# Attention tiles of a fused two-layer kernel: the order of the fc1 and fc2 blocks on the tensor engine, from the third fc2 step on

## The chip, the cores and the metric

One core of one Trainium2 chip. The metric is the device time of one execution in microseconds, lower is better. The kernel before takes 2746.04 us, the median of three runs (2744.83 to 2759.59).

## What is computed

The input is (4, 384, 56, 56) in fp32. Layer 0 is a residual block with group norm, four depthwise convolutions, a sampled value tensor and a projection; the change does not touch it. Layer 1 is a second residual block on group-normed tokens, and its MLP part is where the change sits:

```python
xn = (xs - mu) / jnp.sqrt(var + EPS) * ln_g + ln_b
mid = jax.nn.silu(xn @ fc1_w + fc1_b) @ fc2_w + fc2_b     # 384 -> 1536 -> 384
qkv = (xs @ qkv_w)...                                     # 8 heads of 48
attn = jnp.einsum('bhld,bhle->bhde', k, v)                # q and k normalised
o = 0.5 * v + 1.0 / math.pi * jnp.einsum('bhld,bhde->bhle', q, attn)
o = o / jnp.linalg.norm(o, axis=-1, keepdims=True)
out = (o + mid) @ proj_w + proj_b
```

## The kernel before

The core works through four images (b = 0 to 3). Each image has a stage for keys and values and then seven attention tiles (t = 0 to 6) of 448 tokens; tile n = 7 b + t. Six tiles of images 0 to 2 and all seven of image 3 go through the function `tile`; the seventh of images 0 to 2 goes through `last_tile`, which also holds the output stage of layer 0 for the next image. So there are 25 executions of `tile` and 3 of `last_tile`.

Precision is kept by three passes: each fp32 operand is split into a high part (suffix H, rounded by ScalarE, ACT) and a low part (suffix L, the remainder, by VectorE, DVE), and a product is high times high, high times low, low times high (`three_pass`, lines 784 to 786, one matmul each).

The MLP of a tile is cut into twelve hidden chunks j of 128 (JC = 12). For each chunk:

- `fc1(n, j)` on the tensor engine (PE): nine matmuls into PSUM bank j % 2, from XRH and XRL. It first waits until S of step j - 2 has read that bank (semaphore `s_s`).
- `silu(n, j)` on ACT: S, one of two buffers, after fc1 step j and after the low split of step j - 2; then SH, the high part, one of three buffers, which must wait until fc2 step j - 3 has read it (semaphore `f2`).
- `split_s(n, j)` on DVE: SL, the low part, after SH.
- `fc2(n, j)` on PE: nine matmuls from SH and SL, three into each of banks 2, 3 and 4, in which all twelve steps are summed. It waits for SH and SL of step j.

PE runs fc1 ahead of fc2. `tile` issues fc1 steps 0 to 2, then fc2(0), fc1(3), fc2(1), fc1(4), fc2(2), fc1(5), and then a loop over i = 3 to 11. Between the blocks stand the small steps of the next tile, `pre` (transposes of X, the query matmuls, the query norms, the attention products), the transposes `turn_o` and `turn_unit`, and at i = 9 the output projection `proj` (27 matmuls), which sums into the same banks as fc2. `PRE` says at which i the steps of `pre` stand: the query norms (`query_norms`, 24 matmuls of 8 columns, line 1166) at i = 6, the attention products (`attend`, line 1180) at i = 7 and 8. At i = 5 stands `turn_o` (line 1235).

ACT and DVE run their own orders, written out by hand in the same way: silu steps among the norms, the query copies (line 1748), the copies MH of attended values (line 1772), and on DVE the splits among eight taps for each half of a convolution channel block (line 2395), the low parts ML (line 2369) and the head-wise scaling QQ (line 2345). Waits are on counting semaphores; each engine stops at the first instruction whose wait is not met.

The fc2 loop, word for word, is in the diff below.

Of the kernel before, what the change touches and what calls it, by code (L numbers as in the profile page):

```python
# [73 lines left out]
def build(nc, d, out):  # L74
# [22 lines left out]
    with ctx:  # L97
# [262 lines left out]
        def conv_unit(t, h):  # L360

            return 2 * t + h
# [387 lines left out]
        def _(pe):  # L750
# [31 lines left out]
            def three_pass(o, wh, wl, xh, xl, first, stop):  # L782

                mm(o, wh, xh, start=first, stop=False)  # L784
                mm(o, wh, xl, start=False, stop=False)  # L785
                return mm(o, wl, xh, start=False, stop=stop)  # L786
# [185 lines left out]
            def image(b, nxt):  # L972
# [79 lines left out]
                def key_bank_free(u):  # L1052

                    pe.wait_ge(s["k_ev"], HEAD + b * KVB + 3 * (KVT - 1) + u + 1)

                def value_bank_free(u):

                    pe.wait_ge(s["v_ev"], HEAD + b * KVB + 3 * (KVT - 1) + u + 1)

                def offset_dots():  # L1060

                    pe.wait_ge(s["gelu"], (b + 2) * KC)
                    for t in range(STRIPS):
                        for k in range(KC):
                            last = mm(bank[7][0:TK, 2 * t:2 * t + 2], GE[:, k, t * TK:(t + 1) * TK], woff2c[:, k, :],
                                      start=(k == 0), stop=(k == KC - 1))
                    last.then_inc(s["dots"], 1)
# [93 lines left out]
                def query_norms(n, p):  # L1161
                    pe.wait_ge(s["q_ev"], n * KC + KC)
                    pe.wait_ge(s["qq"], n * KC + KC)
                    for u in range(SUB):
                        for k in range(KC):
                            last = mm(bank[p][0:TS, u * NH1:(u + 1) * NH1], QQ[:, k * T + u * TS:k * T + (u + 1) * TS],  # L1166
                                      hsel[:, k, :], start=(k == 0), stop=(k == KC - 1))
                    last.then_inc(s["qs_mm"], 1)

                def attend(n, u):  # L1170

                    if u == 0:
                        pe.wait_ge(s["q_ev"], n * KC + KC)
                    if u == 2:
                        pe.wait_ge(s["qn_s"], n + 1)
                    if u == 3:
                        pe.wait_ge(s["o_sc"], n * SUB + 1)
                    p = bank[(5, 6, 7, 5)[u]]
                    for k, (lo, hi) in enumerate(WIN):
                        last = mm(p[0:TS, lo:hi], Q[:, k, u * TS:(u + 1) * TS], AB[:, WOFF[k]:WOFF[k] + hi - lo],  # L1180
                                  start=(k == 0), stop=(k == KC - 1), skip_group_check=True)
                    last.then_inc(s["qa_mm"], 1)

                def fc1(n, j):
                    if j == 0:
                        pe.wait_ge(s["xrl"], n + 1)
                        pe.wait_ge(s["xrh"], n + 1)
                    pe.wait_ge(s["s_s"], HEAD + n * JC + (j - 1))
                    p = bank[j % 2][:, 0:T]
                    for k in range(KC):  # L1190
                        last = three_pass(p, W1H[:, k, j * P:(j + 1) * P], W1L[:, k, j * P:(j + 1) * P],
                                          XRH[:, k, :], XRL[:, k, :], k == 0, k == KC - 1)
                    last.then_inc(s["f1"], 1)

                def fc2(n, j, first):
                    pe.wait_ge(s["sl"], HEAD + n * JC + j + 1)
                    pe.wait_ge(s["sh"], n * JC + j + 1)
                    if j == 0 and not first:
                        pe.wait_ge(s["y_s"], HEAD + n * KC)
                    for o in range(KC):  # L1200
                        last = three_pass(bank[2 + o][:, 0:T], W2H[:, j, o * P:(o + 1) * P], W2L[:, j, o * P:(o + 1) * P],
                                          SH[:, j % 3, :], SL[:, j % 3, :], j == 0, j == JC - 1)
                    last.then_inc(s["f2"], 1)
# [11 lines left out]
                def turn_unit(t, h, i):  # L1215

                    c = conv_unit(t, h)
                    if i == 0:
                        pe.wait_ge(s["va"], taps_done(b, t, h))
                        pe.wait_ge(s["vt_ev"], VTT + b * (KC * 8) + c * 4)  # L1220
                    if i == 3:
                        pe.wait_ge(s["vt_ev"], VTT + b * (KC * 8) + c * 4 + 1)
                    for j in range(VU[i]):
                        last = tr(bank[VTB[i]][0:TS, j * P:(j + 1) * P], AC[h][:, (VU0[i] + j) * TS:(VU0[i] + j + 1) * TS], ident[:, :])
                    last.then_inc(s["vtp"], 1)

                def turn_o(n, last):

                    pe.wait_ge(s["o_fin"], n + 1)
                    if not last:  # L1230
                        pe.wait_ge(s["q_ev"], n * KC + 2 * KC)
                        pe.wait_ge(s["qq"], n * KC + 2 * KC)
                    for k in range(KC):
                        for u in range(SUB):
                            last = tr(bank[CB[k]][:, u * TS:(u + 1) * TS], V[:, u, k * P:(k + 1) * P], ident[0:TS, 0:TS])
                        last.then_inc(s["ot_mm"], 1)
# [26 lines left out]
                def tile(n, t):  # L1263
                    first, last = t == 0, t == STRIPS - 1
                    before = nxt and 1 <= t <= KC
                    if first:
                        key_bank_free(3)
                    fc1(n, 0)
                    if first:
                        value_bank_free(3)  # L1270
                        query_norms(n, 3)
                    fc1(n, 1)
                    fc1(n, 2)
                    if first:
                        if nxt:
                            offset_dots()
                        pe.wait_ge(s["qn_s"], n + 1)
                        pe.wait_ge(s["q_ev"], n * KC + KC)
                        pe.wait_ge(s["qq"], n * KC + KC)
                    fc2(n, 0, first)  # L1280
                    if first:
                        pe.wait_ge(s["ab_s"], b + 1)
                        attend(n, 0)
                        attend(n, 1)
                    if before:
                        for i in range(3):
                            turn_unit(t - 1, 1, i)
                    fc1(n, 3)
                    if before:
                        turn_unit(t - 1, 1, 3)  # L1290
                    if first:
                        if nxt:
                            pe.wait_ge(s["off_put"], HEAD + b + 2)
                        attend(n, 2)
                        attend(n, 3)
                    fc2(n, 1, first)
                    fc1(n, 4)
                    pe.wait_ge(s["o_sc"], n * SUB + SUB)
                    if before:
                        pe.wait_ge(s["vt_ev"], VTT + b * (KC * 8) + conv_unit(t, 0) * 4)  # L1300
                    if last:
                        turn_o(n, last)
                    else:
                        pre(n + 1, t + 1, 1)
                    fc2(n, 2, first)
                    fc1(n, 5)
                    for i in range(3, JC):
                        if i == 5 and not last:
                            turn_o(n, last)
                        elif not last and i in PRE:  # L1310
                            for step in PRE[i]:
                                pre(n + 1, t + 1, step)
                        if i == 9:
                            proj(n)
                        fc2(n, i, first)
                        if i + 3 < JC:
                            fc1(n, i + 3)
                        if nxt and t < KC and i == 9:
                            pe.wait_ge(s["o_sc"], (n + 1) * SUB + SUB)
                            for v in range(3):  # L1320
                                turn_unit(t, 0, v)
                        if nxt and t < KC and i == 10:
                            turn_unit(t, 0, 3)
# [39 lines left out]
                for t in range(STRIPS - 1):  # L1363
                    tile(n0 + t, t)
# [1230 lines left out]
```

## Time and profile before

| | |
|---|---|
| Median of three runs | 2746.04 us (2744.83 to 2759.59) |
| Profiled execution, its own time | 2760.41 us |
| Its span (first to last instruction) | 2758.5 us |
| PE busy | 2680.7 us, 97% |
| PE weight loads busy (beside the matmuls) | 2438.1 us, 88% |
| DVE busy | 1979.2 us, 72% |
| ACT busy | 1169.1 us, 42% |
| POOL (GpSimd) busy | 658.1 us, 24% |
| Mean granted clock of PE | 0.97 |

A view of the trace is read like this: times are in us from the start of the span, matmuls overlap their neighbours, so the time that a block takes is the distance from its first start to the next block's first start, not the sum of durations. In brackets stands the idle time of the engine before an instruction and what ended it.

### The profile page before, as it was taken

To read this page: it belongs to the slowest core of one execution; us is meant where nothing else is said; L and a number is where in the kernel's file an instruction comes from. 1 tells how busy PE (TensorE), PEld (TensorE's weight loads), DVE (VectorE), ACT (ScalarE), POOL (GpSimd) and SP (SyncE) were. 2 spreads that over 40 slices of the span, in tenths; PEclk is the share of its full clock that TensorE was granted. 3 is DMA by queue.
4 is the path that set the end of the run, shared out by engine and by line. 5 is a ranking of instruction groups with operands and counts; after the bars stand their busy time and mean duration, and the time that the engine had idled before them with its cause. 6 is when DMAs were issued, how large, how long until landed. Compare 5 with 4: busy or idle time off the path is not lost.

```text
span 2758.5 us, 36700 instructions
## 1 busy us (share of the span) xinstructions
PE 2680.7 (97%) x14382; PEld 2438.1 (88%) x14382; DVE 1979.2 (72%) x2513; ACT 1169.1 (42%) x2035; POOL 658.1 (24%) x219
## 2 busy tenths in 40 slices
PE   6998799999999999999999999999999999999999
PEld 4556799999998999999998999999998899999998
DVE  5989786988886685988886685988887634444442
ACT  3432465444442375444442266444442254333332
POOL 0020142222232043222223042322224033212210
PEclk9998899999999999999999999999999999999999
DMA  5257632433337742333437742333337732121110
GB/s 227 60 146 270 207 119 83 115 104 115 103 110 230 247 133 76 103 103 106 121 108 214 253 151 88 103 103 103 103 106 212 254 97 71 44 54 47 44 44 31
DMA packets 208248, 345.51 MB, mean 125 GB/s; under 512 B 24272, under 2 KB 191824, under 8 KB 205392
## 3 DMA queue, kind: packets, MB, share of 16 engines
q1 hardware_dynamic: 182048, 309.87, 34.5%
q10 hardware_dynamic: 21552, 14.05, 3.5%
q0 software_dynamic: 4480, 19.27, 2.5%
q8 instruction: 115, 1.88, 0.3%
q14 instruction: 53, 0.43, 0.1%
HBM read 239.59 MB, written 103.56 MB: 124 GB/s over the span
## 4 chain that ended last, share of the span: by engine, by line
PE 80%; DMA 5%; issue 5%; DVE 4%; POOL 3%; ACT 2%; SPq 0%; ACTq 0%; DVEq 0%; POOLq 0%
PE bank L784 17%; PE bank L785 17%; PE bank L786 17%; PE bank L989 4%; PE bank L991 4%; PE bank L990 4%; PE bank L830 3%; PE bank L1012 3%; PE bank L1180 3%; DMA X0Q<-in_x 2%; PE bank L1166 2%; POOL rq L706 2%; PE bank L1124 1%; DMA r_scr<-rr 1%; DVE AC L2395 1%
## 5 line engine op out<-in xcount | busy, mean ns | idle before, releaser
L1754 ACT ACTIVATE S<-bank,b1p 128x448 f32<-128x448 f32 x336 | 212.4, 632 | 825.5 <-PE bank L786 798.0
L2395 DVE SCALAR_TENSOR_TENSOR AC<-XV,wfold,AC 128x1568 f32<-128x1568 f32 x288 | 530.1, 1846 | 11.6 <-ACT AC L1786 9.0
L784 PE MATMUL bank<-SH,W2H 128*128 128x448 f32 x1008 | 389.6, 387 | 0.2
L784 PE MATMUL bank<-XRH,W1H 128*128 128x448 f32 x1008 | 377.3, 374 | 1.5 <-ACT S L1754 1.3
L786 PE MATMUL bank<-SH,W2L 128*128 128x448 f32 x1008 | 374.8, 372 | 0.0
L785 PE MATMUL bank<-SL,W2H 128*128 128x448 f32 x1008 | 374.0, 371 | 0.0
L785 PE MATMUL bank<-XRL,W1H 128*128 128x448 f32 x1008 | 373.5, 371 | 0.0
L786 PE MATMUL bank<-XRH,W1L 128*128 128x448 f32 x1008 | 371.4, 368 | 0.0
L706 POOL TENSOR_TENSOR rq<-qn,nhalf 112x32 f32<-112x32 f32 x28 | 181.9, 6497 | 464.2 <-DVE qn L2334 464.2
L2364 DVE TENSOR_TENSOR SL<-S,SH 128x448 fp32r<-128x448 f32 x336 | 207.2, 618 | 86.7 <-ACT SH L1757 86.7
L710 POOL TENSOR_TENSOR ro<-on,nhalf 112x32 f32<-112x32 f32 x28 | 180.1, 6433 | 299.6 <-DVE on L2355 299.5
L698 POOL TENSOR_TENSOR rk<-kn,nhalf 128x16 f32<-128x16 f32 (+1 forms) x64 | 172.6, 2712 | 260.6 <-DVE kn L2177 260.6
L989 PE MATMUL bank<-WKVH,XH 128*128 128x384 f32 (+1 forms) x600 | 207.0, 345 | 12.0 <-DVE XL L2034 10.7
L784 PEld LDWEIGHTS bank<-XRH,W1H 128*128 128x128 f32 x1008 | 193.8, 192 | 18.7 <-ACT S L1754 2.1
L786 PEld LDWEIGHTS bank<-XRH,W1L 128*128 128x128 f32 x1008 | 192.6, 191 | 17.3
L1757 ACT ACTIVATE SH<-S 128x448 fp32r<-128x448 f32 x336 | 194.3, 578 | 31.7 <-ACT S L1754 1.1
L786 PEld LDWEIGHTS bank<-SH,W2L 128*128 128x128 f32 x1008 | 194.5, 193 | 14.2
L785 PEld LDWEIGHTS bank<-XRL,W1H 128*128 128x128 f32 x1008 | 193.1, 192 | 15.1
L784 PEld LDWEIGHTS bank<-SH,W2H 128*128 128x128 f32 x1008 | 193.6, 192 | 14.4 <-DVE SL L2364 1.3
L785 PEld LDWEIGHTS bank<-SL,W2H 128*128 128x128 f32 x1008 | 194.6, 193 | 12.7 <-issue 0.9
L991 PE MATMUL bank<-WKVH,XL 128*128 128x384 f32 (+1 forms) x600 | 201.6, 336 | 0.0
L990 PE MATMUL bank<-WKVL,XH 128*128 128x384 f32 (+1 forms) x600 | 201.5, 336 | 0.0
(227 smaller groups left out, 5160.8 us busy)
## 6 DMA issues: line engine op xcount, KB each, us to landing
XV<-in_xp SPq DMA_DIRECT2D x36, 870.0 KB, 6.8
XC<-in_xp SPq DMA_DIRECT2D x13, 1682.0 KB, 10.9
CQ<-q_scr SPq DMA_DIRECT2D x28, 672.0 KB, 6.1
CX<-in_x SPq DMA_DIRECT2D x28, 672.0 KB, 5.8
x_scr<-CX SPq DMA_DIRECT2D x28, 672.0 KB, 6.4
X<-x_scr SPq DMA_DIRECT2D x28, 672.0 KB, 4.2
V<-v_scr SPq DMA_DIRECT2D x28, 672.0 KB, 7.0
Y<-x_scr SPq DMA_DIRECT2D x28, 672.0 KB, 4.8
```

What stands on the lines that cost most here:

```text
L706: pool.tensor_tensor(rq[:, :], qn[:, :], nhalf[0:TS, :], ALU.pow).then_inc(s["rq_s"], 1)
L710: pool.tensor_tensor(ro[:, :], on[:, :], nhalf[0:TS, :], ALU.pow).then_inc(s["ro_s"], 1)
L784: mm(o, wh, xh, start=first, stop=False)
L785: mm(o, wh, xl, start=False, stop=False)
L786: return mm(o, wl, xh, start=False, stop=stop)
L989: mm(p, xh, WKVH[:, k, c0:c0 + C], start=(k == 0), stop=False)
L990: mm(p, xh, WKVL[:, k, c0:c0 + C], start=False, stop=False)
L991: last = mm(p, xl, WKVH[:, k, c0:c0 + C], start=False, stop=(k == KC - 1))
L1754: fn(S[:, j % 2, :], bank[j % 2][:, 0:T], ACT.Silu, bias=b1p[:, j:j + 1]).then_inc(s["s_s"], 1)
L1757: fn(SH[:, j % 3, :], S[:, j % 2, :], ACT.Copy).then_inc(s["sh"], 1)
L2364: tt(SL[:, j % 3, :], S[:, j % 2, :], f(SH[:, j % 3, :]), ALU.subtract).then_inc(s["sl"], 1)
L2395: stt(o, XV[h][:, ky:ky + HR, kx:kx + W], wfold[:, kind, k, 3 * ky + kx:3 * ky + kx + 1], o, ALU.mult, ALU.add).then_inc(s["va"], 1)
```

## The change

In the loop over i the two blocks change places: fc1 step i + 3 is issued before fc2 step i instead of behind it. That holds for i = 3 to 8, where an fc1 step exists, so for six pairs in each of the 25 executions of `tile`. `last_tile` keeps its order. The other engines' orders, all buffers and all waits stay.

```diff
@@ -1312,9 +1312,9 @@
                                 pre(n + 1, t + 1, step)
                         if i == 9:
                             proj(n)
-                        fc2(n, i, first)
                         if i + 3 < JC:
                             fc1(n, i + 3)
+                        fc2(n, i, first)
                         if nxt and t < KC and i == 9:
                             pe.wait_ge(s["o_sc"], (n + 1) * SUB + SUB)
                             for v in range(3):
```

## Rows read from the trace of the kernel before

**Rows 1.** The page: busy time of PE, and the span in 40 slices

```profile
PE 2680.7 (97%) x14382; PEld 2438.1 (88%) x14382; DVE 1979.2 (72%) x2513; ACT 1169.1 (42%) x2035; POOL 658.1 (24%) x219
...
PE   6998799999999999999999999999999999999999
...
PEclk9998899999999999999999999999999999999999
```

**Rows 2.** Groups by line of PE: busy us, mean ns, idle before, releaser

```profile
L784 PE MATMUL bank<-SH,W2H 128*128 128x448 f32 x1008 | 389.6, 387 | 0.2
L784 PE MATMUL bank<-XRH,W1H 128*128 128x448 f32 x1008 | 377.3, 374 | 1.5 <-ACT S L1754 1.3
L1180 PE MATMUL bank<-AB,Q 128*112 128x144 f32 (+1 forms) x672 | 105.4, 306 | 1.3 <-DVE QQ L2345 1.0
L1166 PE MATMUL bank<-hsel_s,QQ 128*112 128x8 f32 x672 | 68.5, 240 | 2.2 <-DVE ML L2369 2.2
```

**Rows 3.** Waits of the weight loads: us, times, longest

```profile
PEld bank L784 <- ACT S L1754: 2.1, 2, 1.0
...
PEld bank L784 <- DVE SL L2364: 1.3, 3, 0.5
```

**Rows 4.** Timeline of PE, third tile of image 0: start, us, instruction

```profile
665.75 0.37 PE L784 MATMUL bank<-XRH,W1H 128*128 128x448 f32 x1
...
667.61 0.36 PE L784 MATMUL bank<-XH,WQH 128*128 128x448 f32 x1
...
671.21 0.36 PE L784 MATMUL bank<-SH,W2H 128*128 128x448 f32 x1
...
673.01 0.37 PE L784 MATMUL bank<-XRH,W1H 128*128 128x448 f32 x1
...
674.87 1.31 PE L1235 MATMUL bank<-ident_s,V 112*128 112x112 f32 x12
675.95 0.45 PE L784 MATMUL bank<-SH,W2H 128*128 128x448 f32 x1
```

**Rows 5.** Timeline of ACT in the same tile, around steps 5 and 6

```profile
662.02 0.64 ACT L1754 ACTIVATE S<-bank,b1p 128x448 f32<-128x448 f32 x1 [3.32 <-PE bank L786]
...
667.81 0.64 ACT L1754 ACTIVATE S<-bank,b1p 128x448 f32<-128x448 f32 x1 [2.60 <-PE bank L786]
668.54 0.58 ACT L1757 ACTIVATE SH<-S 128x448 fp32r<-128x448 f32 x1
...
669.61 0.55 ACT L1748 ACTIVATE Q<-bank 128x448 f32<-128x448 f32 x1 [0.49 <-PE bank L786]
```

**Rows 6.** Timeline of PE in the last tile of image 3

```profile
2719.95 0.36 PE L784 MATMUL bank<-SH,W2H 128*128 128x448 f32 x1
...
2721.75 0.37 PE L784 MATMUL bank<-XRH,W1H 128*128 128x448 f32 x1
```

**Rows 7.** Timeline of ACT in the last tile of image 3, steps 4 to 6

```profile
2715.32 0.63 ACT L1754 ACTIVATE S<-bank,b1p 128x448 f32<-128x448 f32 x1 [2.35 <-PE bank L786]
...
2720.15 0.64 ACT L1754 ACTIVATE S<-bank,b1p 128x448 f32<-128x448 f32 x1 [2.23 <-PE bank L786]
...
2723.81 0.64 ACT L1754 ACTIVATE S<-bank,b1p 128x448 f32<-128x448 f32 x1 [2.35 <-PE bank L786]
```

**Rows 8.** Timeline of DVE in that tile: the split of step 6

```profile
2725.15 0.62 DVE L2364 TENSOR_TENSOR SL<-S,SH 128x448 fp32r<-128x448 f32 x1 [3.03 <-ACT SH L1757]
```

**Rows 9.** PE in four stretches behind query norms: us, busy (instructions), granted clock, DMA share, GB/s

```profile
481.30:486.61 5.31, 5.31 (x20) 0.68 0.50 164
614.63:619.95 5.32, 5.32 (x21) 0.68 0.52 156
746.24:749.96 3.72, 3.72 (x21) 1.00 1.01 339
2675.52:2680.81 5.29, 5.29 (x20) 0.68 0.00 0
```

**Rows 10.** Line 1166: who waited for the query norms, and its shape

```profile
L1166 PE MATMUL bank<-hsel_s,QQ x672: 170/243/263, 431.7 to 2675.4; 128*112 128x8 f32 x168
...
  DVE ML L2369: 5.8, 7
```

## The prediction

> **What bounds the kernel now.** I read the page first. PE is busy for 97% of the span, every slice from the sixth on is at nine tenths or more, and so is the clock row from the sixth on [rows 1]. So time can only come from three places: PE standing idle, PE at the lower clock, or PE doing less work. The groups by line say how little idle time there is around the moved blocks. Before the 1008 first-pass matmuls of fc2 PE was idle for 0.2 us in all, before those of fc1 for 1.5 us, 1.3 of it for S, over 28 tiles [rows 2]. A modelled busy time can hide a wait, so I looked at starts. In the third tile of image 0 fc2(4) starts at 671.21, fc1(7) at 673.01 and the transposes at 674.87 [rows 4]: nine matmuls in 1.80 us (0.200 each) and in 1.86 us (0.207 each). The same 1.80 stands in the last tile, from 2719.95 to 2721.75 [rows 6], where nothing else is going on. A hidden wait would show as a longer step, and these are alike. The weight loads waited 1.3 us for SL and 2.1 us for S, in five places [rows 3].
>
> Then I read what feeds PE. ACT sits idle before most silu steps because PE has not finished fc1, 3.32 and 2.60 us in the third tile [rows 5], 2.2 to 2.4 us each time in the last one [rows 7]. DVE in the last tile waits 3.03 us for SH [rows 8]. The feeders wait for PE, not PE for them.
>
> **The change, part by part.** *Work.* Nothing is added or removed: 6 pairs in 25 tiles, 150 pairs, change places, 18 matmuls each, with the same loads, waits and signals. No DMA is issued by PE, and none on another queue waits for an fc2 step inside the loop: the store of the output waits for step 11, and its place is the same. Cost in PE work: 0.
>
> *Seams.* After small matmuls the first wide one takes longer, and now that is fc1's. The step behind the query norms without a slow clock, from 746.24 to 749.96, is fc2 and then fc1 in 3.72 us [rows 9]. Plain blocks are 1.80 and 1.82 to 1.86, so the seam costs some 0.1 us once. It stays once per group of small matmuls, whichever block follows. No price for fc1 in that place was taken out of these rows. I bound it from 0 to 0.1 us more or less on the groups ahead of a pair, five in a tile without a wide query block directly before it at most, so 125 x 0.1 = 12.5 us at the outermost to either side. I take 0, since the fc2 seam is a cost of changing from small to wide matmuls and both kinds of block are the same shape.
>
> *The new lead and its wait.* fc1(i+3) now starts where fc2(i) started, one block (1.8 us) sooner. It needs S(i+1), which reads its bank. In the last tile, the densest, fc1(6) would start at 2719.95, where S(4) ended at 2715.32 + 0.63 = 2715.95: 4.0 us to spare. fc1(7) would start 3.66 us later, at 2723.61 (a pair is 1.80 + 1.86), against S(5) at 2720.15 + 0.64 = 2720.79: 2.8 us to spare [rows 6, 7]. From step 6 on S itself moves up with fc1, so the room grows again to some 4.6 us. In the third tile fc1(7) would start at 671.21 and S(5) ended at 662.66 [rows 4, 5]: 8.6 us. New wait: 0.
>
> *The room of fc2.* S(6) starts 0.2 us behind fc1(6), so in the last tile at about 2722.0, not 2723.81. SH(6) must wait for fc2(3), which now ends at 2723.61, so it starts about 2723.8 and ends 2724.4. SL(6) takes 0.62 and ends at 2725.0, where it ended at 2725.77 [rows 7, 8]. fc2(6) starts one block later than before. So the split is 0.7 us earlier and its reader 1.86 us later: 2.6 us more room for fc2. It is room that nobody used: at best it takes away the waits for SL (1.3 us) [rows 3].
>
> *What is queued behind the hold.* ACT now stands at SH(i+3) until fc2(i) ends. fc1(i+4) always comes after fc2(i) and takes 1.86 us, and SH(i+3) needs 0.2 + 0.58 us, so ACT is back 1.1 us before the next silu can start. At i = 3 the query copy stands behind it: it waited for its matmuls, ending at 669.41, and started at 669.61 [rows 4, 5], where SH(6) now ends before 668.5. The same holds for the attended copies behind silu(7), whose transposes begin at 674.87. They can be 0.7 us earlier, never later. For DVE a split comes 0.7 us earlier or at the same time. The waits of the query norms for ML (2.2 us) and of the attention for QQ (1.0 us) [rows 2, 10] may shrink, so the other gain is 0 to 3.2 us.
>
> The Trainium skill, "TensorE: Matmul & The Clock Gate", section on the engine queue depths, says that ScalarE and VectorE take their instructions strictly in order, and that speaks against the change: everything behind a held SH is late. The trace's order of ACT in this tile agrees with it [rows 5]. By that rule alone the price would be the 1.8 us of the hold at each pair, and the 2.60 us that ACT idled before S(6) cover it.
>
> *The clock.* Behind the query norms PE fell to the lower of its two levels (1.2 GHz, against 2.4) for most of two blocks: the pair took 5.31, 5.32 and 5.29 us at a mean granted clock of 0.68, against 3.72 us at 1.00 in another tile [rows 9]. So a fall costs 1.6 us. Of the 24 tiles that carry these norms in their loop, 16 show a fall and 8 none, the same instructions in both (the first and the last of the 16 stand there). The change puts fc1 ahead of the norms' fc2 but neither moves the norms nor changes what PE did before them in amount. I take the number as it is: 0.
>
> *Pace of fc1.* fc1 blocks came at 1.86 us in some stretches and, as in the 3.72 us pair, at about 1.82 in others. I counted 98 of the first and 182 of the second among those behind another wide block. All slow would be 182 x 0.04 = +7 us, all fast -4 us. I take 0.
>
> **Sum.** Work 0, seams 0, new wait 0, shrinking waits 0 to -4.5 us (1.3 + 2.2 + 1.0). The three first tiles, whose norms come after a long chain over POOL, hold the larger ML waits, and the change does not shorten that chain, so I take -1. The profiled execution would go from 2760.4 to 2759.4 us. It lies 14 us above the median, at the top of the three runs, so the same difference against the median gives 2745 us.
>
> **Rivals.**
>
> *A. ACT's hold or the new bank wait reaches PE (slower).* The place is fc1(7) of each tile. For: ACT is in order and holds longer; against: 2.8 us to spare in the tightest tile. It decides only if S(5) ends more than 2.8 us later than it did, and it is not itself moved, or if the 1.1 us behind the hold plus that room is eaten. Were it to be 1 us too late in every tile, 25 us: 2770 us (+0.9%). Below 0.55 us a tile it stays within 0.5%. Chance 0.04.
>
> *B. The waits all go (faster in sign).* Less SL, ML and QQ waiting, -4.5 us: 2741.5 us (-0.2%). It can't reach 0.5% from these rows, as PE has no more idle time there. Chance 0.15, within "same".
>
> *C. The falls of the clock change in number.* For: the norms are followed by a fall in 16 tiles and not in 8, so a small shift of the whole schedule may decide. With all 24 falling, 8 x 1.6 = +13 us: 2758 us (+0.5%). With 8, -13 us: 2732 us (-0.5%). With none, -26 us: 2719 us. Chance of more than four falls either way 0.15, split evenly; beyond 0.5% some 0.06. The Trainium skill, same page, section on what is actually happening, says that the gate's watching runs freely and is not tied to the kernel's start, so that the number of slow matmuls differs between executions. By that rule the median would move by a part of the spread of the runs, 14.8 us, with or without the change. The trace agrees as far as one execution can, with its 16 and 8.
>
> *D. The seams or the pace of fc1 shift.* -12.5 to +12.5 us and -4 to +7 us at the ends, from above: 2730 to 2765 us. Chance of more than 5 us 0.08.
>
> **How the numbers follow.** The forecast, 2740 to 2751 us, has 0.58, and B, which lies at its lower edge, 0.15. A has 0.04, C 0.15, D 0.08. The likeliest is 2745 us. The range takes in C to about eight falls more or less, D's pace, and the upper runs of the spread: 2733 to 2759 us. A measurement of this kernel tells about 0.5%, 14 us, from no change. Faster by more than that takes C downward or D's seams together with B: 0.06. Slower takes A, C upward or D: 0.08. Within: 0.86.
>
> **What the profile of the changed kernel would show.** Idle time before the fc1 group for S should stay under 3 us; more than 15 us means A. The starts in the last tile should read fc1 then fc2 with the same 1.86 and 1.80. S should start nearly a block earlier in the loop, SH some 0.7 us earlier, and ACT should show a new idle time before SH ended by PE, of about a block less 0.8 us. SL should be no later. The query norms should be followed by falls in some 12 to 20 tiles. The prediction is wrong if the fc1 step behind small matmuls takes clearly over 1.96 us, if the blocks' spacing changes, or if the tiles get longer with no wait to show for it.

## The result, and the profile after

The changed kernel takes 2744.29 us, the median of 20 runs (2737.43 to 2759.82). The kernel before takes 2756.19 us, the median of 20 runs (2743.79 to 2763.24), 10 us more than the three runs that stood ahead of the prediction and that are among the 20. The ratio is 0.9968, 95% interval 0.9956 to 0.9981: 0.3% faster, some 9 us (the two medians lie 11.9 us apart). The forecast was 2745 us, no change within 0.5%, and -1 us for the change itself. That the change stays within 0.5% came out, but its size is some nine times what was said. That the time came out too, to within 1 us, was luck: the start of the sum was 10 us too low and the gain was taken some 10 us too small, and the two errors cancel. One run further down, of the kernel that is changed in three tiles only, took 3540.77 us at a mean clock of 0.70, and it is left out of that kernel's figures.

The page of the changed kernel, with its busy line, and PE and its clock in 40 slices:

```profile
span 2747.1 us, 36700 instructions
...
PE 2674.4 (97%) x14382; PEld 2439.4 (89%) x14382; DVE 1978.7 (72%) x2513; ACT 1168.3 (43%) x2035; POOL 661.4 (24%) x219
...
PE   6998799999999999999999999999999999999999
...
PEclk9998899999999999999999999999999999999999
```

The work is the same, 14382 matmuls [rows 1], and PE is busy for 6.3 us less.

Its groups by line on PE, columns as in [rows 2]:

```profile
L784 PE MATMUL bank<-XRH,W1H 128*128 128x448 f32 x1008 | 387.2, 384 | 0.7 <-ACT S L1754 0.7
L784 PE MATMUL bank<-SH,W2H 128*128 128x448 f32 x1008 | 379.4, 376 | 0.1
L1180 PE MATMUL bank<-AB,Q 128*112 128x144 f32 (+1 forms) x672 | 103.0, 303 | 1.1 <-DVE QQ L2345 1.1
L1166 PE MATMUL bank<-hsel_s,QQ 128*112 128x8 f32 x672 | 68.8, 241 | 2.1 <-DVE ML L2369 2.1
```

The reader is to see that fc1 did not take up a wait: 0.7 us for S where it was 1.3. The longer first matmul behind small ones now lies with fc1 (384 ns against 374) and no longer with fc2 (376 against 387).

The view by line of ACT, before:

```profile
L1754 ACT ACTIVATE S<-bank,b1p 128x448 f32<-128x448 f32 x336 | 212.4, 632 | 825.5 <-PE bank L786 798.0 <-DMA r_scr<-rr 24.7 <-DVE SL L2364 2.7
L1757 ACT ACTIVATE SH<-S 128x448 fp32r<-128x448 f32 x336 | 194.3, 578 | 31.7 <-ACT S L1754 1.1
```

and in the changed kernel:

```profile
L1754 ACT ACTIVATE S<-bank,b1p 128x448 f32<-128x448 f32 x336 | 212.6, 633 | 686.0 <-PE bank L786 625.1 <-DMA r_scr<-rr 35.3 <-DVE SL L2364 25.3
L1757 ACT ACTIVATE SH<-S 128x448 fp32r<-128x448 f32 x336 | 194.3, 578 | 139.8 <-PE bank L786 117.7 <-ACT S L1754 1.1
```

Before, ACT sat idle for 798.0 us before S with PE as the cause, and for 31.7 us before SH, none of it for PE. So the silu steps do start earlier and the hold of SH is there, 118 us in all. The wait of S for SL has grown from 2.7 to 25.3 us: ACT now runs so far ahead that DVE's low split two steps back frees the buffer of S last. It costs PE nothing that the profile shows, as fc1 waits 0.7 us for S.

PE and ACT in the last tile of image 3 of the changed kernel, fc2(3) at 2710.54 and fc2(4) at 2714.17 as landmarks:

```profile
2708.72 0.36 PE L784 MATMUL bank<-XRH,W1H 128*128 128x448 f32 x1
...
2710.54 0.36 PE L784 MATMUL bank<-SH,W2H 128*128 128x448 f32 x1
...
2712.34 0.36 PE L784 MATMUL bank<-XRH,W1H 128*128 128x448 f32 x1
...
2714.17 0.36 PE L784 MATMUL bank<-SH,W2H 128*128 128x448 f32 x1
```

```profile
2710.74 0.64 ACT L1754 ACTIVATE S<-bank,b1p 128x448 f32<-128x448 f32 x1 [0.52 <-PE bank L786]
2712.54 0.58 ACT L1757 ACTIVATE SH<-S 128x448 fp32r<-128x448 f32 x1 [1.16 <-PE bank L786]
2714.37 0.64 ACT L1754 ACTIVATE S<-bank,b1p 128x448 f32<-128x448 f32 x1 [1.25 <-PE bank L786]
```

SH stands for 1.16 us and then starts 0.20 us behind the end of fc2(3), and ACT is back 1.25 us before the next silu. The working had 1.1 us. And fc1 takes 1.82 and 1.83 us, from 2708.72 to 2710.54 and from 2712.34 to 2714.17, where all twelve fc1 blocks of this tile took 1.86 before.

The pair behind the query norms, in four of the 24 tiles of the changed kernel, columns as in [rows 9]:

```profile
482.20:487.49 5.29, 5.29 (x21) 0.68 0.48 151
549.47:553.18 3.71, 3.71 (x20) 1.00 0.26 105
...
1736.52:1742.98 6.46, 6.46 (x19) 0.54 0.42 138
...
2666.12:2669.83 3.71, 3.71 (x20) 1.00 0.00 0
```

13 of the 24 pairs show the lower clock, against 16 before.

### The profile page after: what moved, and what is told of

It is laid out like the page before. It is cut to its first block, busy times and chain, and to the rows that moved or that the text cites. A ratio compares the mean times of both kernels' runs of the same rounds, so it can differ in the third digit from the quotient of the medians.

```text
span 2747.1 us, 36700 instructions
## 1 busy us (share of the span) xinstructions
PE 2674.4 (97%) x14382; PEld 2439.4 (89%) x14382; DVE 1978.7 (72%) x2513; ACT 1168.3 (43%) x2035; POOL 661.4 (24%) x219
## 4 chain that ended last, share of the span: by engine, by line
PE 83%; issue 6%; DVE 4%; POOL 3%; DMA 2%; ACT 2%; SPq 0%; ACTq 0%; DVEq 0%; POOLq 0%
PE bank L784 18%; PE bank L786 18%; PE bank L785 18%; PE bank L989 4%; PE bank L991 4%; PE bank L990 4%; PE bank L830 3%; PE bank L1180 3%; PE bank L1012 3%; PE bank L1166 2%; PE bank L1124 1%; POOL ro L710 1%; POOL rq L706 1%; PE bank L1224 1%; PE bank L1235 1%
## 5 line engine op out<-in xcount | busy, mean ns | idle before, releaser
L2395 DVE SCALAR_TENSOR_TENSOR AC<-XV,wfold,AC 128x1568 f32<-128x1568 f32 x288 | 530.0, 1845 | 11.4 <-ACT AC L1786 8.8
L784 PE MATMUL bank<-XRH,W1H 128*128 128x448 f32 x1008 | 387.2, 384 | 0.7 <-ACT S L1754 0.7
L784 PE MATMUL bank<-SH,W2H 128*128 128x448 f32 x1008 | 379.4, 376 | 0.1
L786 PE MATMUL bank<-XRH,W1L 128*128 128x448 f32 x1008 | 377.3, 374 | 0.0
L785 PEld LDWEIGHTS bank<-XRL,W1H 128*128 128x128 f32 x1008 | 194.4, 193 | 13.5
```

The source lines that it names most:

```text
L2395: stt(o, XV[h][:, ky:ky + HR, kx:kx + W], wfold[:, kind, k, 3 * ky + kx:3 * ky + kx + 1], o, ALU.mult, ALU.add).then_inc(s["va"], 1)
```

## The experiments

Two theories stood at first. By one (L) the gain lay in the three tiles with an output stage. In the first two profiles PE waited there for the sampled values (VS) 13.1 us before and 4.7 us after, and one such tile took 111.4 us before and 104.4 after:

```profile
PE bank L902 <- DVE VS L1996: 13.1, 8, 3.0
```

```profile
PE bank L902 <- DVE VS L1996: 4.7, 3, 1.6
```

By the other (C) it lay in the number of falls of the clock. Behind the first experiments two more were put up. By W the gain is time in which PE waited for DVE's products ML and QQ, which now come earlier relative to PE. By P it is the pace of the fc1 blocks, 1.82 us instead of 1.86.

### Each kernel again

The edit is none: the kernel before against itself, and the changed kernel a second time.

> The kernel before, unchanged, run against itself, to see how far two sets of runs and two profiles of one program lie apart. Theory L (the time came from the three tiles with an output stage, whose length hangs on how long the X0Q load takes): those tiles are 104 to 112 us long here too, and their sum moves the time. Theory C (the falls of the clock behind the query norms, 16 of 24 tiles before and 14 or so after): ratio 1.000, the number of falls between 12 and 20. A ratio outside 0.997 to 1.003 would mean that the 0.3% of the change is not distinguishable from chance.

Measured: 2762.59 us (12 runs), ratio 1.0011, 0.9997 to 1.0024, so 0.3% can be told from chance.

> The changed kernel again. If the 0.9968 measured first is real, the ratio is 0.995 to 0.999. Theory L expects the three tiles with an output stage to be 5 to 10 us shorter in sum than in the profile of the kernel before. Theory C expects a higher mean clock than the kernel before in the same call, by 0.001 to 0.003, and output-stage tiles as long as before on average.

Measured: 2745.76 us (6 runs), ratio 0.9953, 0.9939 to 0.9967. The gain is real, 0.3 to 0.5%. The mean clock was 0.9725 over its runs, 0.9723 over those of the kernel before taken beside them, and 0.9727 over the 20 runs of the changed kernel in the first comparison. Theory C had asked for 0.001 to 0.003 more than the kernel before.

The two new profiles speak against theory L as the whole of it. The three output-stage tiles took 103.3, 103.5 and 103.9 us in the second profile of the kernel before, less than in the first one of the changed kernel (111.2, 104.4, 105.3). Their length differs by 7 us between executions of one program. The 25 executions of `tile`, added up from the first start of one to that of the next, took 1656 and 1664 us before and 1653 and 1653 us after. So in the first pair of profiles 3 of the 11 us of difference lie in these tiles and nearly all the rest in the output-stage tiles (10 us); in the second pair all of it lies in the 25 tiles.

PE in the second profile of the kernel before, by line:

```profile
L784 PE MATMUL bank<-XRH,W1H 128*128 128x448 f32 x1008 | 377.5, 374 | 3.9 <-DVE XRL L2311 2.5 <-ACT S L1754 1.3
L1180 PE MATMUL bank<-AB,Q 128*112 128x144 f32 (+1 forms) x672 | 102.3, 300 | 3.9 <-DVE QQ L2345 3.9
L1166 PE MATMUL bank<-hsel_s,QQ 128*112 128x8 f32 x672 | 69.6, 242 | 3.0 <-DVE ML L2369 3.0
```

The same lines in the second profile of the changed kernel:

```profile
L784 PE MATMUL bank<-XRH,W1H 128*128 128x448 f32 x1008 | 386.1, 383 | 2.7 <-DVE XRL L2311 1.4 <-ACT S L1754 1.3
L1180 PE MATMUL bank<-AB,Q 128*112 128x144 f32 (+1 forms) x672 | 103.2, 303 | 0.9 <-DVE QQ L2345 0.7
L1166 PE MATMUL bank<-hsel_s,QQ 128*112 128x8 f32 x672 | 68.9, 241 | 2.1 <-DVE ML L2369 2.1
```

The reader is to see that PE waited 6.9 us for QQ and ML (3.9 + 3.0) in this execution of the kernel before, and 2.8 us in the changed one (0.7 + 2.1). The first pair of profiles shows nothing of the kind: 3.2 us before (1.0 + 2.2) and 3.2 us after (1.1 + 2.1). The wait for XRL is one wait each time, ahead of the first tile of image 3, and is not laid to the lead: the changed kernel with DVE made light, further down, has 1.8 us of it.

A steadier measure is all idle time of PE in stops of over 0.15 us, from the first tile to the end: 24.7 and 24.2 us before, 17.7 and 18.8 us after. So the changed kernel has 5 to 7 us less of it in either pair. In the first pair it went from the waits for VS, in the second from those for QQ, ML and XRL.

### The change in part of the tiles

```diff
-                        fc2(n, i, first)
-                        if i + 3 < JC:
-                            fc1(n, i + 3)
+                        swap = not nxt          # image 3 only; second kernel: nxt and t == STRIPS - 2
+                        if swap and i + 3 < JC:
+                            fc1(n, i + 3)
+                        fc2(n, i, first)
+                        if not swap and i + 3 < JC:
+                            fc1(n, i + 3)
```

> The blocks change places in image 3 only: 7 of 25 tiles, 42 of 150 pairs, none of them ahead of an output stage. Theory L: no gain, ratio 0.999 to 1.001. Theory C and any theory of a gain at each pair: 42/150 of 0.32%, a ratio of 0.9991, too small to tell from L by the time alone; the tiles of image 3 in the profile would be shorter by 0.35 us each.

Measured: 2756.72 us, ratio 0.9992, 0.9979 to 1.0004.

> The blocks change places only in the tile before each output stage (t = 5 of images 0 to 2): 3 tiles, 18 pairs. Theory L: this is where the transfers and gathers of the output stage are started, so most of the gain is here, ratio 0.996 to 0.998, with output-stage tiles shorter by 2 to 3 us each. Theories of a gain at each pair: 18/150 of the gain, ratio 0.9996 to 1.000.

Measured: 2758.02 us (11 runs), ratio 0.9994, 0.9981 to 1.0007. The least gain that theory L expected, 0.998, lies just outside. Both agree with a gain that is spread over the tiles. The profile of this kernel, in which 22 of 25 tiles have the old order, is like the second one of the kernel before:

```profile
PE bank L1180 <- DVE QQ L2348: 3.8, 7, 0.8
```

What is not ruled out is that the new order in all tiles shortens the waits for VS in the output stage. They were 13.1, 4.7, 8.4 and 10.0 us in the profiles of the kernel before and of these two, and 4.7 and 5.3 us in those of the changed kernel; the further kernels below with the new order in all tiles and full taps had 4.8, 4.8 and 6.2. No run was made to settle it.

### The first three pairs, and the last three

The same edit with `swap = i <= 5`, and with `swap = i >= 6`.

> Only the pairs of steps 3 to 5 change places, 75 of 150. They lie ahead of the copies MH, the splits ML and the query norms. Theory W (the gain is the waits of PE for DVE's QQ and ML and other late feeders, which DVE's 0.7 us of lead shortens): the lead is gained at steps 3 to 5 and used at step 7 and 8, so most of the gain is here, ratio 0.996 to 0.998. Theory P (the gain is the pace of fc1 blocks, 1.82 instead of 1.86 us in the loop behind the norms): little of it, ratio 0.9985 to 1.000. Theory C (fewer falls of the clock behind the norms): the block between which the norms stand is already changed ahead of them, so half of it or more.

Measured: 2749.48 us, ratio 0.9978, 0.9962 to 0.9993.

> Only the pairs of steps 6 to 8 change places, 75 of 150, from the query norms on. Theory W: little, ratio 0.9985 to 1.000. Theory P: most of its part, as the slow pace is taken up behind the norms and the attention products and is then kept into the next tile: 3 to 5 us, ratio 0.998 to 0.999, and blocks of 1.86 us in the first steps of the following tiles should be gone. Theory C: the block that the fall lies in is fc1 instead of fc2, so the rest of it.

Measured: 2752.97 us, ratio 0.9981, 0.9968 to 0.9994. The halves are alike, and their sum agrees with the whole (-0.22 and -0.19%, against -0.32 and -0.47%). W expected less of the second half than that. The profiles show two different effects. From the end of ML to the start of the query norms lay 0.73 and 0.43 us on average over 24 tiles in the two profiles of the kernel before, 1.30 and 0.98 us in those of the changed one, 1.03 with the first pairs alone and 0.46 with the last alone. So the lead comes from the first pairs, and with it the waits of PE for QQ shrink: 1.7 us with the first pairs alone, 4.5 us with the last alone. The time by which fc1 matmuls behind another wide matmul exceed a start every 0.200 us, summed over the 25 tiles, was 11.8 and 11.4 us before, 9.8 and 9.2 after, 10.2 with the first pairs alone and 9.7 with the last alone. That part is gained by either.

### The query norms woven into the block ahead of them

The 24 small matmuls are issued as 6, 6 and 12 behind the first, second and third three wide ones of the block in front. The core of the edit:

```diff
+                        def norms(g):
+                            if g == 0:
+                                pe.wait_ge(s["ml"], (n + 1) * KC)
+                            query_norms(n + 1, 7, ((0,), (1,), (2, 3))[g])
+
+                        woven = norms if i == 5 and not last else None
                         if i + 3 < JC:
                             fc1(n, i + 3)
-                        fc2(n, i, first)
+                        fc2(n, i, first, woven)
```

In the order of before `woven` goes to `fc1(n, i + 3)`, the block that stands there.

> The order of before, but the 24 small matmuls of the query norms are woven into the fc1 block ahead of them (three wide, six small, three wide, six small, three wide, twelve small) in the 24 tiles. If the run of small matmuls is what the clock falls for, the 16 falls of 1.6 us go and some 0.2 us a tile for two more seams comes: -25 + 5 = -20 us, ratio 0.993. If it is not, ratio 1.000 to 1.003. With the falls gone in both orders, theory C expects this kernel and its twin in the changed order to be equal; theories W and P expect the twin still 0.2 to 0.4% faster.

Measured: 2780.75 us, ratio 1.0098, 1.0079 to 1.0117. Slower by 24 to 27 us (by the medians and by the ratio), which none of the theories had.

> The changed order with the query norms woven into the fc2 block ahead of them in the same way. Theory C (the changed order has fewer falls): equal to its twin in the order of before. Theories W and P: 0.2 to 0.4% faster than the twin, so ratio 0.989 to 0.991 against the kernel before if the falls go, else 0.995 to 0.998.

Measured: 2745.15 us, ratio 0.9957, 0.9942 to 0.9972. In this form the two orders lie 36 us apart. Waits of PE, us in all, times and longest, first in the order of before with the norms woven:

```profile
PE bank L1167 <- DVE ML L2384: 19.3, 23, 1.9
```

and in the changed order with the norms woven:

```profile
PE bank L1167 <- DVE ML L2384: 7.7, 7, 1.9
```

Woven, the norms start 1.2 us sooner and ask for ML at once. In the order of before ML then holds the matmuls in 23 of 24 tiles, in the changed order in 7. The weight loads, which start before their matmuls, waited in 23 tiles in the order of before and in 13 in the changed one. First the order of before:

```profile
PEld bank L1167 <- DVE ML L2384: 27.9, 23, 2.3
```

and in the changed order:

```profile
PEld bank L1167 <- DVE ML L2384: 12.6, 13, 2.3
```

That shows the lead directly. One such wait in the order of before:

```profile
550.95 0.76 PE L1167 MATMUL bank<-hsel_s,QQ 128*112 128x8 f32 x6 [0.39 <-DVE ML L2384]
552.25 0.66 PE L1167 MATMUL bank<-hsel_s,QQ 128*112 128x8 f32 x6
553.45 1.25 PE L1167 MATMUL bank<-hsel_s,QQ 128*112 128x8 f32 x12
```

The waits for ML differ by 11.6 us, a third of the 36. The mean clock was 0.9678 over the runs of the first and 0.9753 over those of the second, and 0.0075 of 2750 us is some 20 us (estimated as in the section on the prediction, by one less the clock). So a shorter run of small matmuls does not by itself bring fewer slow stretches: with it the clock was lower than in the kernel before (0.9720 in the runs beside these) where PE stopped for ML, and higher where it mostly did not. That the stops bring the slow stretches fits this and was not tested apart. What the additional seams cost was not measured.

### DVE made light

Each tap of the convolution on DVE works on 2 of its 28 rows; the other 26 are left out. This concerns images 0 to 2.

```diff
+                        o = o[:, 0:2, :]
-                        stt(o, XV[h][:, ky:ky + HR, kx:kx + W], ...
+                        stt(o, XV[h][:, ky:ky + 2, kx:kx + W], ...
```

> The order of before, with each convolution tap of DVE in the tiles of images 0 to 2 cut to 2 of its 28 rows (288 instructions of 1.85 us become short; the rest of the convolution is left out), so that DVE is never late in them. The twin with the changed order goes with it. Theory W (late ML and QQ of DVE hold PE): the waits behind attention and norms in images 0 to 2 go already here, some 5 to 9 us, ratio 0.995 to 0.998, and the twin is then at most 3 to 5 us faster than this one. Theory P (pace of fc1): the twin is faster by its part of 2 to 4 us. If the twin is still 11 us faster, the late feeder is not DVE.

Measured: 2741.34 us, ratio 0.9938, 0.9914 to 0.9963.

> The changed order with the same cut of DVE's taps. Theory W: 3 to 5 us below its twin, not 11, as only ACT's part of the lead and the pace of fc1 are left. A theory in which the gain is in the order on PE alone (pace, falls of the clock): 8 to 12 us below the twin, as with the full taps.

Measured: 2738.00 us, ratio 0.9926, 0.9903 to 0.9950. With DVE light the order of before alone gains 13.5 us, more than the change does, and the change then adds 3.3 us (2741.34 - 2738.00), where it is worth 9 to 13 us with the full taps. From the spread of the six runs each, 3.3 us may be anything from -1 to 8. PE by line, light, order of before:

```profile
L1180 PE MATMUL bank<-AB,Q 128*112 128x144 f32 (+1 forms) x672 | 103.0, 304 | 0.0
L1166 PE MATMUL bank<-hsel_s,QQ 128*112 128x8 f32 x672 | 68.7, 241 | 0.8 <-DVE ML L2369 0.8
```

and light, changed order:

```profile
L1180 PE MATMUL bank<-AB,Q 128*112 128x144 f32 (+1 forms) x672 | 102.5, 303 | 0.0
L1166 PE MATMUL bank<-hsel_s,QQ 128*112 128x8 f32 x672 | 70.2, 243 | 0.0
```

No wait for QQ is left in either, and none or 0.8 us for ML. All idle time of PE from the first tile on is 16.8 and 16.6 us, and the 25 tiles take 1650 us in both profiles, so with DVE light the order no longer makes a difference there. W holds in kind: most of the change's gain is time that goes with DVE being late. The cut makes all that DVE does in images 0 to 2 earlier, so it shows DVE as the late feeder, and not which of its products. The order of before gained more than W had said (ratio 0.9938, where 0.995 to 0.998 was expected), and more than the 7.6 us of idle time that went; its mean clock was 0.9742, against 0.9727 of the kernel before beside it, which is some 4 us. The part that stays agrees with P, as the excess of the fc1 spacing was 12.2 and 9.4 us in these two.

### Two further orders

The weave in all tiles but the first of an image, where ML hangs on a chain over POOL:

```diff
-                        woven = norms if i == 5 and not last else None
+                        woven = norms if i == 5 and not first and not last else None
```

> The changed order with the query norms woven into fc2(5), but not in the first tile of an image, where ML is late by the chain over POOL and weaving cost 1.1 us more waiting. Against the weave in all tiles (0.9957) 3 to 4 us less: ratio 0.994 to 0.995, and 2740 to 2743 us. If the weave gains nothing by itself, 0.9955.

Measured: 2744.31 us, ratio 0.9949, 0.9929 to 0.9969. The interval holds both the weave in all tiles and the change alone, so it is not shown to beat the changed kernel.

The new order from the second step on:

```diff
+                    if not first:
+                        fc1(n, 4)
                     fc2(n, 1, first)
-                    fc1(n, 4)
+                    if first:
+                        fc1(n, 4)
```

and the same for `fc1(n, 5)` and `fc2(n, 2, first)`.

> The changed order extended: in all tiles but the first of an image, fc1(4) is issued ahead of fc2(1) and fc1(5) ahead of fc2(2) too, 44 more pairs. Theory W (a lead gained once): no further gain, ratio 0.995 to 0.997, as ML and QQ are used late in the tile and the lead at step 3 is what counts. A theory in which each pair gains 0.07 us: 3 us more, ratio 0.994. Slower than 0.997 would mean that the wait of fc1(4) for S(2), which comes late behind the copies of X, reaches PE.

Measured: 2751.05 us, ratio 0.9976, 0.9959 to 0.9992. No further gain, so it is not so much a pair. From the end of ML to the query norms lay 0.97 us in its profile, no more than with the change alone. By the expectation a ratio above 0.997 would have meant that fc1 waits for S; its profile has 1.3 us of that, no more than the kernel before, but it is of the fastest of the 12 runs. Whether this kernel is slower than the change was not settled.

## Why the prediction came out as it did

*Work.* Right: 14382 matmuls in both.

*Seams.* Taken as 0, and 0. Behind small matmuls fc1 takes 1.90 to 1.96 us. Summed over the 25 tiles, what wide blocks behind small ones took beyond 0.200 us a matmul was 18.2 and 17.8 us before, 18.0 and 17.8 after.

*New wait.* Right: fc1 waited 0.7 us for S in one profile and 1.3 us in the other, against 1.3 us before.

*The hold.* Right in mechanism and nearly in size: SH stands for 1.16 us, and ACT is back 1.25 us before the next silu. The working had 1.1 us for the second, because it left out the 0.2 us from the end of fc1 to the start of S. The sentence that ACT and DVE are 0.7 us earlier and never later held on average: ML's lead over the norms grew by 0.55 to 0.57 us (0.73 to 1.30, 0.43 to 0.98). That S would wait for SL, 25.3 us, was not in the working.

*Room of fc2.* Right in direction and worth nothing, as said.

*Shrinking waits.* This is the term that was mis-sized. It read "shrinking waits 0 to -4.5 us", and took -1. All idle time of PE from the first tile on went down by 7.0 and 5.4 us in the two pairs of profiles. By another way, with DVE light the order matters by 3.3 us and with full DVE by 9 to 13, so 6 to 10 us of the change go with DVE's lateness. Two things were wrong in the bound. It counted the waits for QQ, ML and SL only, and rival B said that PE has no more idle time there; but the profile had 24.7 us of idle time in the tiles and stages behind the first norms, 13.1 of them for VS, which were not priced. And it was read from one execution, which had 3.2 us of waits for QQ and ML. The second execution of the same program had 6.9 us for them, and its 25 tiles took 8 us more. The same goes for the three runs: their median lay 10 us below that of 20.

*The three first tiles.* The reason given for taking -1, that the larger ML waits stand in the first tiles and stay, was true for ML (2.2 to 2.1 us). In the second pair of profiles the waits for QQ in the other tiles went from 3.9 to 0.7 us; in the first pair they stayed (1.0 and 1.1).

*Pace of fc1.* Taken as 0 within +7 to -4 us; it was -2 us. In the kernel before I counted 98 fc1 blocks behind a wide block at 1.86 us; in the changed one 37, nearly all behind a query block. The prediction had said that the starts in the last tile would keep 1.86, and had named a change of the blocks' spacing as a sign that it is wrong. That sign came, at the size of 2 us; why the pace changed stays open.

*The clock.* Taken as 0. The profiles had 16 and 17 falls of 24 before, 13 and 14 after. By the falls that is 3 x 1.6 = 5 us; by the mean clock of all runs, 0.9723 against 0.9727 (the time lost is about one less the clock, times 2750 us), it is 1.1 us. The second rests on far more executions. That fewer small stops of PE also make fewer falls would fit the mean clocks of 0.9742 with DVE light and of 0.9678 with the norms woven in the order of before, but was only argued.

Rival A did not come: no wait of fc1 for S. Rival B named the mechanism and put its end at -4.5 us; it was rated at 0.15 and belonged first, and its end was too near. Less idle time of 5 to 7 us, pace 2 and clock 1 us add up to 8 to 10, against 9 to 13 measured. How the idle time divides among QQ, ML and VS, whether VS belongs to the change at all, and what shorter waits do to the clock stays open.

## What to carry to other kernels

An engine that idles 1% of its span can still be held by a feeder, in stops of under a microsecond, at the places where the feeder's other work meets it. Look for them in more than one execution before a bound is put on them: here one profile had 3 us for QQ and ML and the next 7. The median of three runs was 10 us off in the same way, and a forecast that hits from such a start has shown nothing. A reordering that gives no new room that is used to the instructions that it moves can give a lead to a third one that stands behind them in another engine's queue, and that lead is the thing to price. To see whether a margin is thin, ask for it 1 us earlier: with the norms woven, two orders whose margin differs by 0.6 us showed waits for ML in 23 and in 7 of 24 tiles, 11.6 us apart.

## What had not been expected of the hardware

Blocks of nine equal matmuls on one bank come at 1.82 us or at 1.86 us, up to a whole tile on end, with nothing waiting: 1.86 throughout the last tile before, 1.82 after. Blocks over three banks come at 1.80 in both. What sets the pace was not found.

The clock fell behind a stretch in which PE was not idle, 24 matmuls of 8 columns in 2.3 us (only in the first tile of images 0 to 2 did 0.7 us of waiting stand before it), and the second profile of two equal programs had another set of tiles with a fall. The Trainium skill, "TensorE: Matmul & The Clock Gate", section on oscillation, tells of the gate by idle gaps of the engine; in the other tiles there was none here, and the traces show a fall in 13 to 17 of 24 such stretches.
